# Expert stage: plain scatters, a residual loaded ahead, and the first product as three float32r matmuls

## The reference, cut to what matters

```
buf  = zeros(E, C, D).at[idx, pos].set(x)            # E = 8 experts, C = 1280 places, D = 128
hmid = relu(einsum('ecd,edf->ecf', buf, w1) + b1)    # 128 -> 512: the first expert product
ybuf = einsum('ecf,efd->ecd', hmid, w2) + b2         # 512 -> 128: the second
y    = nan_to_num(ybuf[idx, pos] * (prb * kept))     # back to the token's place
out  = t + y                                         # then to channels-first (B, 128, 32, 32)
```

## Time and profile before

| | |
|---|---|
| time, median of 3 runs | 1735.05 us (1733.45 to 1736.13) |
| span of the profiled execution | 1754.3 us, the only time that the profile gives of it |
| first transpose of the expert stage on PE | 1547.0 us |
| first and last accumulating scatter begin | 1571.1 and 1722.8 us |
| busy share over the whole span | PE 89%, DVE 76%, ACT 58%, POOL 39% |
| mean TensorE clock granted | 0.943 of full speed |

### The profile page before, as it was taken

One profiled execution on the slowest core, in us unless ns is written; L12 is line 12 of the kernel. 1 busy time (PEld: TensorE's weight loads), 2 busy tenths in 40 slices (PEclk: granted clock), 3 DMA queues, 4 the chain that ended last, 5 costly groups with the idle time before them and its releaser, 6 DMA issues.

```text
span 1754.3 us, 24814 instructions
## 1 busy us (share of the span) xinstructions
PE 1566.4 (89%) x8374; PEld 748.2 (43%) x8374; DVE 1338.5 (76%) x2758; ACT 1015.3 (58%) x1939; POOL 676.3 (39%) x1027
## 2 busy tenths in 40 slices
PE   4768999999999999999999999999988988889983
PEld 2523423443453344434433454335433323457762
DVE  4278898789878987998798978996889863735770
ACT  1402666766856685777565767675766686134332
POOL 4112301005541364135414541453245364328882
PEclk8876999999999999999999999999999999989995
DMA  3172451153216221622153215320452111135437
GB/s 79 50 202 96 158 157 33 34 150 102 79 47 182 71 79 47 175 78 79 47 153 99 79 46 143 97 80 21 139 151 86 39 45 33 42 69 100 75 38 203
DMA packets 131595, 161.50 MB, mean 92 GB/s; under 512 B 18740, under 2 KB 98361, under 8 KB 131470
## 3 DMA queue, kind: packets, MB, share of 16 engines
q1 hardware_dynamic: 112238, 146.95, 28.5%
q0 software_dynamic: 13568, 7.31, 3.1%
q10 hardware_dynamic: 5664, 5.66, 1.0%
HBM read 102.97 MB, written 58.33 MB: 92 GB/s over the span
## 4 chain that ended last, share of the span: by engine, by line
PE 47%; DVE 18%; POOL 12%; ACT 8%; DMA 6%; issue 6%; SPq 2%; another core or an unknown queue 1%; ACTq 1%; POOLq 0%; DVEq 0%
PE bank L1587 8%; PE bank L1556 8%; POOL t_d L1420 7%; PE bank L1511 7%; PE bank L1575 7%; DVE gmax L2193 6%; DVE cmax L2132 3%; PE bank L1430 3%; ACT prob L1946 3%; PE bank L1624 2%; PE bank L1503 2%; DVE ol_tok L2256 1%; PE bank L1614 1%; PE bank L1525 1%; PE bank L1530 1%
## 5 line engine op out<-in xcount | busy, mean ns | idle before, releaser
L1946 ACT ACTIVATE prob<-bank 128x512 f32<-128x512 f32 x1024 | 573.0, 596 | 297.9 <-PE bank L1575 276.8
L2193 DVE TENSOR_REDUCE gmax<-bank 128x1 f32<-128x512 f32 x1024 | 657.3, 683 | 59.7 <-PE bank L1556 50.4
L1556 PE MATMUL bank<-k_stack,q_stack 96*128 96x512 bf16 x1024 | 401.9, 398 | 34.9 <-DVE gmax L2193 19.1
L1575 PE MATMUL bank<-q_stack,k_stack 99*128 99x512 bf16 x1024 | 388.9, 387 | 33.2 <-ACT prob L1946 22.2
L1587 PE MATMUL bank<-prob,v_tok 128*32 128x512 f32 x2048 | 279.0, 618 | 0.0
L1342 POOL TENSOR_TENSOR lprod<-ql_tok,kv_win 128x640 f32<-128x640 f32 x64 | 99.6, 1578 | 371.6 <-DMA ql_tok<-ql_d 353.5
L1556 PEld LDWEIGHTS bank<-k_stack,q_stack 96*128 96x128 bf16 x1024 | 100.6, 99 | 274.3 <-DVE gmax L2193 171.3
L1349 POOL TENSOR_TENSOR lprod<-ls,kv_win 128x640 f32<-128x640 f32 x64 | 81.8, 1299 | 267.2 <-DVE ls L2249 267.2
L1575 PEld LDWEIGHTS bank<-q_stack,k_stack 99*128 99x128 bf16 x1024 | 99.7, 99 | 198.1 <-ACT prob L1946 135.2
L1420 POOL DMA_INDIRECT t_d<-kv_win,token_e x80 | 129.2, 1615 | 53.9 <-DVE kv_win L2535 29.9
L1511 PEld LDWEIGHTS bank<-cv_tok,cprob 128*128 128x128 f32 x960 | 118.7, 199 | 29.8 <-DVE t_tok L2160 16.1
(11 more groups left out here) (274 smaller groups left out, 2370.9 us busy)
## 6 DMA issues: line engine op xcount, KB each, us to landing
kv_win<-kv_d SPq DMA_DIRECT2D x32, 1280.0 KB
kv_d<-lqkv SPq DMA_DIRECT2D x64, 128.0 KB, 2.1
gparts_d<-cprob SPq DMA_DIRECT2D x24, 256.0 KB
gparts_d<-parts SPq DMA_DIRECT2D x24, 256.0 KB
q_stack<-gparts_d SPq DMA_DIRECT2D x32, 192.0 KB, 3.2
k_stack<-gparts_d SPq DMA_DIRECT2D x16, 384.0 KB, 5.4
rows_d<-rows SPq DMA_DIRECT2D x10, 528.0 KB, 4.4
cprob<-rows_d SPq DMA_DIRECT2D x8, 660.0 KB, 4.5
```

What stands on the lines that cost most here:

```text
L1556: mm(max_ps[max_bank(n)][:, :], q_stack[quad][0:KROWS, h, i * P:(i + 1) * P], key_slot(b, quad)[0:KROWS, h, j * HN:(j + 1) * HN], start=Tr ...
L1575: mm(score_ps[n % 2][:, :], key_slot(b, quad)[0:KM, h, j * P:(j + 1) * P], q_stack[quad][0:KM, h, half * HN:(half + 1) * HN], start=True, ...
L1946: nc.scalar.activation(prob[:, g % 2, h, :], score_ps[n % 2][:, :], ACT.Exp).then_inc(exp_made, 1)
L2193: v.tensor_reduce(gmax[:, h, i, j:j + 1], max_ps[max_bank(n)][:, :], AX.X, ALU.max)\
```

## The change

There are four parts.

1. **Plain scatters.** A new DRAM tensor `y_d` takes the experts' results. POOL's 80 scatters write there without accumulating. `y_d` is zeroed early, by 8 further stores of 512 KB on SP beside the zeroing of `rows_d`, since a dropped token must add nothing.
2. **Preloaded residual.** SP loads t2 in 8 transfers of 512 KB during the expert stage into tiles that are free by then. POOL's wait for `t2_out` and `end_t2_out` moves to SP.
3. **Closing pass.** SP and ACT each issue 8 loads of `y_d` (rows of 2 KB, 16 buffers), DVE adds the residual to each piece, PE transposes, ACT copies with a strided output, and SP issues the stores.
4. **First product.** w1 and the tokens are split: ACT writes a part rounded to float32r (`w1h_e`, `xh_e`), DVE subtracts it from the exact value and writes the remainder (`w1l_e`, `xl_e`). Each product is then three float32r matmuls into one bank: high by high, high by low, low by high. `expert_columns(e + 1, 2)` moves behind `expert_result(e, 0)` on PE and on DVE.

```diff
+    y_d = nc.dram_tensor("y_d", [B * N, C], F32).ap()
...
-        x_e = prob[:, :, :, :].rearrange("p a b c -> p (a b c)")[:, 0:CAP]
+        xh_e, xl_e = over_prob("xh_e", CAP, 0), over_prob("xl_e", CAP, CAP)
...
                 sp.dma_start(rows_d[e * NT * P:(e + 1) * NT * P, :].rearrange("(p t) r -> p t r", p=P),
                              rows[:, :, :]).then_inc(scratch_zeroed, 16)
+                if e < B:
+                    sp.dma_start(y_d[e * N:(e + 1) * N, :].rearrange("(p t) c -> p t c", p=P),
+                                 rows[:, :, 0:C]).then_inc(scratch_zeroed, 16)
...
+            def t2_rows(b):
+                sp.dma_start(t2_home[b].rearrange("p (k n) -> p k n", k=2), t2_v[b]).then_inc(t2_in, 16)
...
             for e in range(2, E):
                 expert_rows(e)
                 expert_weights(e)
+                t2_rows(e - 2)
+            for b in range(E - 2, B):
+                t2_rows(b)
...
-            with sp.Fori(0, 2 * B // ENDS) as r:
-                for k in range(ENDS):
-                    sp.wait_ge(fin_full[k], r)
-                    sp.dma_start(fin_tok[k], t2_v[r, k]).then_inc(fin_in[k], 16)
+            for n in range(0, ENDS, 2):
+                sp.dma_start(fin_y[n], y_v[n]).then_inc(fin_in[n // 2], 16)
+            for n in range(ENDS):
+                sp.wait_ge(fin_made, n + 1)
+                sp.dma_start(out_b[n // 2, :, n % 2 * HN:(n % 2 + 1) * HN], fin_cm[n]).then_inc(fin_out, 16)
...
-            pool.wait_ge(t2_out, (B - 1) * 16)
-            pool.wait_ge(end_t2_out, 2 * 16)
...
-                    pool.indirect_dma_start(t2_d, bass.IndirectOffsetOnAxis(ap=token_e[e % 2][:, i:i + 1], axis=0),
-                                            y_e[e % 2][:, i, :], None, bounds_check=last_token, oob_is_err=False,
-                                            compute_op=ALU.add).then_inc(ey_out[e % 2], 16)
+                    pool.indirect_dma_start(y_d, bass.IndirectOffsetOnAxis(ap=token_e[e % 2][:, i:i + 1], axis=0),
+                                            y_e[e % 2][:, i, :], None, bounds_check=last_token, oob_is_err=False)\
+                        .then_inc(ey_out[e % 2], 16)
...
-                        mm(bank[2 + u % 4][:, 0:n], w1_e[e % 2][:, f * P:(f + 1) * P], x_e[:, lo:lo + n],
-                           start=True, stop=True).then_inc(eh_full, 1)
...
+                        mm(bank[2 + u % 4][:, 0:n], w1h_e[e % 2][:, w], xh_e[:, t], start=True, stop=False)
+                        mm(bank[2 + u % 4][:, 0:n], w1h_e[e % 2][:, w], xl_e[:, t], start=False, stop=False)
+                        mm(bank[2 + u % 4][:, 0:n], w1l_e[e % 2][:, w], xh_e[:, t], start=False, stop=True)\
+                            .then_inc(eh_full, 1)
...
+            def expert_weight(e):
+                act.wait_ge(ew1_in[e % 2], e // 2 * 16 + 16)
+                to(w1h_e[e % 2][:, :], w1_e[e % 2]).then_inc(ew1h_made, 1)
...
-                    to(x_e[:, lo:lo + n], bank[c % 2][:, 0:n]).then_inc(ext_free, 1)
+                    to(xh_e[:, lo:lo + n], bank[c % 2][:, 0:n]).then_inc(exh_made, 1)
...
+            for n in range(ENDS):
+                act.wait_ge(fin_full, n + 1)
+                to(fin_cm[n].rearrange("c (p t) -> c t p", t=END_T),
+                   bank[n % END_BANKS_N][:, :].rearrange("c (t p) -> c t p", t=END_T)).then_inc(fin_made, 1)
...
+            def expert_columns(e, c):
+                lo, n = XT_CHUNKS[c]
+                dve.wait_ge(exh_made, e * 3 + c + 1)
+                v.tensor_tensor(xl_e[:, lo:lo + n], bank[c % 2][:, 0:n], xh_e[:, lo:lo + n].bitcast(F32), ALU.subtract)\
+                    .then_inc(ext_free, 1)
+
+            def expert_weight(e):
+                dve.wait_ge(ew1h_made, e + 1)
+                v.tensor_tensor(w1l_e[e % 2][:, :], w1_e[e % 2], w1h_e[e % 2][:, :].bitcast(F32), ALU.subtract)\
+                    .then_inc(ew1l_made, 1)
...
+            dve.wait_ge(t2_in, B * 16)
+            for n in range(ENDS):
+                dve.wait_ge(fin_in[n // 2], 32)
+                v.tensor_tensor(fin_y[n], fin_y[n], fin_t2[n], ALU.add).then_inc(fin_sum, 1)
```

More of the change, by code:

```diff
@@ L28 @@
 F32 = mybir.dt.float32
+F32R = mybir.dt.float32r
 BF16 = mybir.dt.bfloat16
@@ L88 @@
 EARLY_BANKS = [0, 4, 5]
-ENDS = 4
+ENDS = 16
+END_BANKS_N = 8
+END_T = 4
 MAX_BANKS = 3
@@ L883, in hybrid_kernel @@
         ext_free = sem("ext_free")
+        exh_made = sem("exh_made")
+        ew1h_made = sem("ew1h_made")
+        ew1l_made = sem("ew1l_made")
         eh_full = sem("eh_full")
@@ L1066, in hybrid_kernel @@
         assert first_loads == FIRST_LOADS, first_loads
+        y_v = y_d.rearrange("(n p t) c -> n p (t c)", p=P, t=END_T)
         block = ctx.enter_context(nc.Block())
@@ new lines, in _ @@
+            expert_weight(0)
+            for c in range(3):
+                expert_columns(0, c)
+            for e in range(E):
+                expert_slots(e)
+                if e + 1 < E:
+                    expert_columns(e + 1, 0)
+                    expert_columns(e + 1, 1)
+                    expert_weight(e + 1)
+                expert_result(e, 0)
+                if e + 1 < E:
+                    expert_columns(e + 1, 2)
+                expert_result(e, 1)
+                expert_result(e, 2)
```

174 lines of the change are left out of this document (99 added, 75 removed).

## The result

The changed kernel took 1713.7 us (median of 4 runs, 1705.72 to 1714.78) beside 1734.25 us for the kernel before on the same chip; the ratio is 0.9861 (0.9837 to 0.9884), 20 to 28 us less. A second set beside other runs of before gave 1709.8 us (5 runs), ratio 0.9842 (0.9821 to 0.9864), 24 to 31 us less. Forecast was 30.2 us less, 1705 us: above the first interval and inside the second.

A forecast was written before the change was run, and what follows sets the result against it. The prediction took TensorE and GpSimd's accumulating scatters as equally binding. The first load of `y_d` 27.4 us earlier and 3.1 us off the closing pass gave 30.5, taken as 30.2 off 1735.05: 1705 us, range 1694 to 1721.

The forecast's parts named there:

- its own case: Whole kernel: TensorE sets a period of 16.8 us for each expert; 1705 us, within 1696 to 1713, chance 0.72.
- rival 1: Expert stage: VectorE becomes the bound, period 18 us; 1712 us, up to 1720 with a late closing pass, chance 0.10.
- The bound before: Expert stage before: TensorE (19.16 us an expert) and GpSimd's scatters (19.2) equally slow; a faster product alone wins nothing.
- the drain: End of expert stage: the last scatter starts 27.6 us after the start of expert 7's products.
- the landing: From the last scatter's start to the first load waiting for it: 2.18 us for a plain scatter, 3.43 before.
- the closing pass: After the last scatter: loads with 2 KB rows cut DMA time to 22.0 us and the pass from 28.0 to 24.9.
- rival 3: First product on TensorE: float32r matmuls cost 0.43 us each, period 23.4 us; time about 1757 us, chance 0.08.
- VectorE's 16.0 us: VectorE's work for one expert: 13.5 us plus 2.5 us of added subtractions, 0.5 us from being late.
- The order on TensorE: Third chunk's transposes moved behind result 0, so TensorE's wait of 0.33 us for ScalarE's copy goes.
- Scatters: GpSimd's plain scatters in the expert stage: 1.28 us each against 1.92, so 12.8 us for an expert.
- rival 2: GpSimd: scatters don't get faster, because of the target or VectorE's work beside them; about 1731 us at 1.92, chance 0.04.
- Rival 4: Still faster: closing pass of 20 us and TensorE's clock up from expert 0's start (3 us); 1690 to 1696, chance 0.06.

The follow-up runs named there:

- e3: The kernel before with only the new product, its remainders and TensorE's new order; accumulating scatters and old closing pass: 1737.96 us, ratio 1.0006 to before.
- e8: The changed kernel with its scatters into `y_d` accumulating again: 1732.62 us, ratio 0.998 to the kernel before.
- e2: The changed kernel with the first product as one float32 matmul again, without rounded parts or subtractions: 1719.49 us, ratio 0.9904 to the kernel before.
- e4: The changed kernel with a second, unread tensor zeroed by eight more stores: 1709.06 us, ratio 0.9841 to the kernel before.
- e6: The changed kernel with one float32r matmul instead of three in each first product, remainders still made: 1696.45 us, ratio 0.977 to the kernel before.
- e10: The changed kernel with four more unread subtractions on VectorE for each expert: 1716.17 us, ratio 0.9887 to the kernel before.
- e12: The changed kernel with two float32r matmuls instead of three in each first product, remainders still made: 1694.41 us, ratio 0.9771 to the kernel before.
- e7: The changed kernel with two more unread subtractions on VectorE for each expert: 1707.88 us, ratio 0.9843 to the kernel before.
- e11: The changed kernel with all three chunks of transposes ahead of the results again, on TensorE alone: 1721.12 us, ratio 0.9922 to the kernel before.
- e9: The changed kernel with 512 byte rows in the closing pass's loads and ScalarE's copies without stride: 1710.0 us, ratio 0.9859 to the kernel before.
- e5: The changed kernel once more, no edit: 1709.8 us, ratio 0.9842 to the kernel before.

## Why the prediction was right, point by point

**The time and the mechanism.** The median of the first set, 1713.7 us, lies 0.7 us above the band that the forecast gave its own case (1696 to 1713) and inside that of rival 1 (1712 to 1720). The time alone can't tell the two apart. The traces can: TensorE has no wait from 1560 to 1690 us, and VectorE waits in each period, so the forecast's own case is the one that came.

**The bound before** holds. e3 shows that a faster product alone wins nothing, as the forecast said, and e8 that accumulating scatters, with all the rest changed, hold the time at 0.998 of before. No run has the plain scatter alone. The nearest is e2, with plain scatters, TensorE's new order and the new closing pass, but the old product: 16.7 us by the ratio, 17.5 from S. Of these, 7.5 us lie between the start of expert 7's products and the last scatter (30.1 us instead of 37.7): that is what the faster scatter takes from the drain. Another 4.6 us come ahead of it, 0.55 from each of six periods and 1.3 from expert 0, with the new order; the landing gives 1.2 and the closing pass 4.1.

**Zeroing costs nothing**: right as far as e4 can tell, which adds eight stores to the eight. No run leaves the eight out of the changed kernel.

**The float32r matmul** was taken at 0.22 us for 512 columns and measured 0.233 (0.12 for 256), so 7.14 us for the products with what follows them, instead of 6.6. It is the largest error in the period, and only one of size: rival 3, with 0.43, is ruled out by the timeline. The transposes took less than taken: 1.09 us for all ten, 0.87 for the first eight. Period 17.02 against 16.8, TensorE without a wait: right.

**VectorE's 16.0 us** was 0.3 too high, since I added lengths: independent operations overlap by 0.08 us each, and four were added. I then gave it 0.5 us of slack by following one chunk through the engines. The trace after shows two waits of VectorE in each period, 0.58 us on average for ScalarE's copy (3.5 us in six) and 0.72 for result 0 (6.8 us, less 2.5 in the drain, in six), and their sum, 1.3, is the slack that e6, e10 and e12 agree on (17.02 - 15.70 = 1.32, and 2.4 - 1.10 = 1.30) and that e7 allows (at least 1.2). Rival 1 (VectorE binds) is ruled out at this load, but it is near: e10 reached it with 2.4 us.

**The order on TensorE** was undersized. The forecast costed the moved third chunk at the 0.33 us wait that it saw before, and e11 shows 1.96 us an expert, 14.9 us over the stage. The wait that the move avoids is not the old one; the change itself lengthens it by VectorE's subtraction. This did not spoil the sum, which rested on a period without a wait. But whoever took the product without TensorE's move would have had 193.4 us from S, no better than the old product with the move (189.8; by the medians 1721.12 and 1719.49 us, with intervals that overlap). The old product without the move was not run beside plain scatters; with the 4.6 us above it would end at about S + 194.4 (an estimate), so the float32r product is worth about 1 us there and 11.3 with the order.

**Scatters** were taken at 1.28 us of pitch. That is the floor (0.97 + 0.30), which every scatter keeps that has no VectorE instruction beside it (5 in the changed kernel, 25 in e2); the mean length over the 80 is 1.03 (the group of line 1454 has 82.5 us for them). In the drain four scatters beside VectorE took 5.81 us instead of 5.12, and since GpSimd was by then a little late already, the last starts 28.7 us after the products of expert 7, not 27.6. This is the mechanism of rival 2, at a tenth of its size. The Trainium skill (SBUF — State Buffer, SBUF: two separate sides) says that GpSimd can't write descriptors while VectorE holds the shared port pair; by that rule the rows above and those of e8 would be its work. They agree in sign, and in e8 the whole stage shows 0.04 us more for each scatter than before. But VectorE's busy share does not set the length: e2 has it busy 71% of a stretch of five periods and scatters of 1.05 us on average, the changed kernel 89% and 1.03. What stands beside a scatter matters more. In the changed kernel all of the 15.2 us that COPY_PREDICATED of 512 columns shares with scatters lies in ones longer than 1.01 us, but only 0.3 of 7.8 us of the multiplication of 512 columns. No run here shows that the port is the cause.

**The closing pass** took 25.05 us, forecast 24.9, with 22.5 us of DMA time, forecast 22.0. e9 confirms both the row size as the reason and that the strided copy of ScalarE, at 0.94 us rather than 0.53, stays hidden. That the length fits so well is in part luck. The same pass took 24.9 to 25.1 us in seven profiles (the changed kernel, e4, e5, e7, e8, e10, e11) and 23.9 in three (e2, e6, e12). The DMA time is 22.5 us in e2 as well (94.4% of 23.89 us). The seven have one transfer of 0.02 MB of code in the pass and the three, which are the programs with the fewest instructions, have none. In the changed kernel it takes 0.3% of 16 engines' 25.05 us, which is 1.2 us if one engine carries it, and its last 2.2 us have a DMA share of 0.04 and 16 GB/s, as if one engine ended late. So the pass without that load is 23.9 us, 1.0 below the forecast. That the code is the cause is argued from these ten profiles; no run moves it.

**The landing** of the last scatter took 2.19 us, forecast 2.18.

**The sum.** From S: expert 1's products at 20.4 (forecast 21.3), six periods of 17.02 (16.8), the drain 28.7 (27.6), the landing as forecast, the pass 25.05 (24.9). That is -0.9 + 1.3 + 1.1 + 0.1 = 1.6, and 178.5 stands against 176.8. The -0.9 is expert 0: its subtraction (0.3), its products at 7.7 us instead of 8.0, and transposes and results at 9.9 instead of 10.2. TensorE starts slow there as forecast, but for less long: the float32r matmuls stand 0.57 to 0.40 us apart up to 1537.5, 4.2 us from S, and 0.23 after, and the granted clock over the 20.4 us is 0.90, which is half speed for 4.1 us; forecast were 6. Rival 4 needed full speed from the start and a pass of 20 us, and neither came. The 28.8 us from S lie above the first set's interval (20 to 28) and inside the second's (24 to 31); the stretch ahead of S scatters by more than the difference, and whether part of it is real stays open.

How the parts combine, by the time from S to the end: before 207.3 to 208.0, the product alone 207.2, scatters with closing pass and order 189.8, all but the plain scatter 203.6, all 178.5. The product is worth 0 to 1 us alone and 11.3 with the rest (12.5 up to the closing pass).

## What to carry to other kernels

When two engines run at the same pace, price each change with the other one made and not made: the product was worth nothing alone and 11 us behind the faster scatter. Slack of an engine is the sum of its waits in one steady period, read from its timeline; a chain followed through lengths gave less than half of it. And when a change puts a step between a producer and a consumer (here a subtraction behind a copy), look for who waits for the buffer in the old order: the move of one chunk was worth 1.96 us an expert, the old wait showed 0.33.

## What the runs showed of the hardware

- At a granted clock of 1.00 a float32r matmul of 512 columns starts every 0.233 us, where a bfloat16 one stands at 0.22 and a float32 one at 0.86; for 256 columns it is 0.12.
- GpSimd needs 1.54 us to issue an accumulating scatter of 128 rows of 512 bytes, and 0.97 us for a plain one. Only scatters with a VectorE instruction beside them are longer, by up to 0.5 us in the kernel before and in e8, and 0.3 in the changed kernel.
- ScalarE's copies of 128x512 from a bank follow each other every 0.94 us when they write with a stride of four elements and every 0.53 without (1.11 to 1.20 and 0.60 us long).
- The same closing pass took 1.1 us longer in the profiles that have 0.02 MB of code loaded in it (seven) than in those that have none (three).
- The same kernel's planned part took 23 us more in one profiled execution than in another, while the stretch behind it repeated within 0.7 us.
